# VectorE's residual between the square sums, masks and first exponentials ahead of O's rounding, the value product next to the following scores

## The reference

```python
x = x + 0.5 * ffn(layernorm(x))
x = x + ttt(layernorm(x))          # a sequential linear memory, here "mid"
x = x + 0.5 * ffn(layernorm(x))
```

```python
def _layer(x, ...):
    h = shift_token(x)
    q, k, v = split(h @ wqkv)                    # 256 -> 3 x 512
    q, k = rotary_xpos(l2norm(q) * qs, l2norm(k) * ksc)
    o = local_attention(q, k, v)                 # own and previous 128 tokens
    x = x + o @ wo
    h = layernorm(shift_token(x)) * lg + lb
    a, g = split(h @ w1 + b1)
    x = x + (a * gelu(g)) @ w2 + b2
```

## Time and profile before

| | us |
|---|---|
| median of 3 runs (2850.06 to 2856.06) | 2854.98 |
| time of the profiled execution | 2850.51 |
| span of the profiled execution, first to last instruction | 2848.6 |
| PE matmul busy | 2547.3 (89%) |
| PE weight load busy | 2224.7 (78%) |
| DVE busy | 1987.4 (70%) |
| ACT busy | 1843.2 (65%) |
| POOL busy | 1528.3 (54%) |
| mean granted TensorE clock, share of full | 0.996 |

### The profile page before, as it was taken

The page is one execution under the profiler, slowest core; times in us unless marked ns, Lnnn a source line. Parts: engine busy times, 40 slices in busy tenths (PEclk is TensorE's granted clock), DMA queues, the critical chain, the costliest instruction groups (busy, mean ns, idle before and its releaser), DMA issues.

```text
span 2848.6 us, 79930 instructions
## 1 busy us (share of the span) xinstructions
PE 2547.3 (89%) x29664; PEld 2224.7 (78%) x29664; DVE 1987.4 (70%) x6533; ACT 1843.2 (65%) x5192; POOL 1528.3 (54%) x1767
## 2 busy tenths in 40 slices
PE   7898888998888898899999888899988888999898
PEld 6787777887777787788767777788777777788778
DVE  6776677676767666677656767676766677777776
ACT  5766666666666666666454666666666666666665
POOL 5565556555555556555213555555564555555654
PEclk9999999999999999999999999999999999999999
DMA  3122011003000000004100000000003000000000
GB/s 112 31 76 72 30 34 46 24 19 109 13 2 2 2 2 24 2 2 173 46 23 25 2 2 2 2 2 2 2 2 108 32 2 17 17 17 17 17 17 24
DMA packets 75954, 82.18 MB, mean 29 GB/s; under 512 B 37552, under 2 KB 61872, under 8 KB 74416
## 3 DMA queue, kind: packets, MB, share of 16 engines
q1 hardware_dynamic: 70176, 75.51, 8.1%
q10 hardware_dynamic: 5392, 1.56, 0.2%
HBM read 49.53 MB, written 26.74 MB: 27 GB/s over the span
## 4 chain that ended last, share of the span: by engine, by line
PE 38%; DVE 19%; ACT 18%; POOL 11%; issue 9%; DMA 4%; SPq 2%; DVEq 0%; ACTq 0%; POOLq 0%
PE bank L1111 6%; PE bank L1113 5%; PE bank L1112 5%; POOL pr L631 5%; PE bank L1222 5%; ACT pT L834 5%; DVE pr L1714 5%; ACT pr L815 4%; PE bank L1147 3%; PE bank L1345 3%; DMA stt<-stt 2%; PE bank L1191 2%; POOL r L626 2%; PE bank L1510 2%; POOL r L618 2%
## 5 line engine op out<-in xcount | busy, mean ns | idle before, releaser
L631 POOL TENSOR_TENSOR pr<-pr,rden 128x384 f32<-128x384 f32 (+1 forms) x512 | 435.9, 859 | 645.3 <-DVE rden L1723 644.6
L815 ACT ACTIVATE pr<-pr,nb 128x192 f32<-128x192 f32 (+1 forms) x1024 | 439.1, 430 | 92.3 <-DVE nb L1714 92.3
L1714 DVE CUSTOM_DVE_ANT_0 pr<-bank,maskb,r 128x192 f32<-128x192 f32 (+1 forms) x1024 | 357.3, 395 | 102.5 <-POOL r L626 59.9
L1111 PE MATMUL bank<-h2T,w 128*128 128x256 f32 x1408 | 405.3, 288 | 10.1 <-DVE h2T L1749 4.8
L1112 PE MATMUL bank<-h2T,w 128*128 128x256 f32 x1408 | 394.8, 280 | 0.0
L1113 PE MATMUL bank<-h2T,w 128*128 128x256 f32 x1408 | 394.8, 280 | 0.0
L1111 PE MATMUL bank<-wqkv,hT 128*128 128x512 f32 x768 | 321.3, 418 | 60.5 <-DVE nb L1714 55.4
L663 POOL TENSOR_TENSOR uTl<-t,uTh 128x256 fp32r<-128x256 f32 x288 | 218.0, 757 | 211.4 <-ACT uTh L911 210.6
L1811 DVE SCALAR_TENSOR_TENSOR t<-bank,b,t 128x256 f32<-128x256 f32 (+1 forms) x384 | 182.8, 480 | 185.2 <-ACT t L896 103.0
L1112 PE MATMUL bank<-wqkv,hT 128*128 128x512 f32 x768 | 304.0, 396 | 0.0
L1113 PE MATMUL bank<-wqkv,hT 128*128 128x512 f32 x768 | 302.8, 394 | 0.0
(11 more groups left out here) (244 smaller groups left out, 7362.9 us busy)
## 6 DMA issues: line engine op xcount, KB each, us to landing
wqkv<-wqkv_split SPq DMA_DIRECT2D x18, 512.0 KB, 6.5
w<-w_split SPq DMA_DIRECT2D x3, 2816.0 KB, 9.6
Y<-in_x SPq DMA_DIRECT2D x8, 512.0 KB, 7.3
out<-Y SPq DMA_DIRECT2D x8, 512.0 KB, 3.6
stt<-stt SPq DMA_DIRECT2D x224, 3.0 KB
h<-out SPq DMA_DIRECT2D x7, 512.0 KB, 5.0
out<-h SPq DMA_DIRECT2D x7, 512.0 KB, 3.0
stt<-stt SPq DMA_DIRECT2D x192, 0.0 KB
```

The lines of the kernel that those rows point to most:

```text
L631: e.tensor_tensor(probs(j, t), probs(j, t), rden[:, 2 * j:2 * j + 2].unsqueeze(2).to_broadcast([P, 2, w]), ALU.mult).then_inc(pn_done, 1)
L815: last = e.activation(probs(j, t)[:, g, :], probs(j, t)[:, g, :], ACT.Exp, bias=nb[:, hd:hd + 1], scale=-1.0, accum_out=den[:, hd:hd + 1])
L1111: e.matmul(out, left[0], right[0], start=first, stop=False)
L1714: m = e.tensor_tensor_reduce(probs(j, t)[:, g, :], bank[j][:, g * 256:g * 256 + w], far, r[:, t, 1, place(hd):place(hd) + 1], FAR, ALU.add ...
```

## The change

No instruction of arithmetic is added or removed. Six edits move calls:

1. ACT: the two copies into `o_sum` become a function `O_first`. It runs ahead of `S(0)` of the next tile as before, but the rounded high part `O` now follows `S(0)`.
2. DVE: `O` (the low part) moves from between `S(0)` and `S(1)` to behind `S(3)`; `LN_moments` of tile 3 moves with it, from behind `S(1)`.
3. DVE: `WO(t-1)`, the residual, moves from behind `A0` to between the square sums of k and of q.
4. PE: `A2` (k and q turned) now runs ahead of `PV` instead of behind it.
5. PE: the table `cuts` is another one. The units in `fill(0)`, `fill(1)` and `fill(2)` were 0, 6 and 6 for t = 0 (5 more stand ahead of `S`, as before), 0, 11 and 6 for t = 1 and 2, and 0, 8 and 9 for t = 3. Now they are 4, 8 and 0, then 4, 13 and 0, and 4, 5 and 8.
6. ACT: `A2` (kT and qT copied) of tile 3 moves ahead of `O` and `H2T`.

```diff
--- before.py
+++ after.py
@@ -834,6 +834,15 @@
                         last = e.activation(pTe[64 * a:64 * a + 64, g::2, :], halves_of[64 * g:64 * g + 64, :, a, :], ACT.Copy)
                 last.then_inc(pt_sb, 1)
 
+            def O_first(L, b, t):
+
+                n = idx(L, b, t)
+                e.wait_ge(o_lo, at(o_lo, 2 * n))
+                e.wait_ge(pv_ps, at(pv_ps, 2 * n + 2))
+                for i in pair:
+                    cols = slice(2 * P * i, 2 * P * i + 2 * P)
+                    e.activation(o_sum[:, cols], bank[O_BANK[0]][:, cols], ACT.Copy).then_inc(o_first, 1)
+
             def O(L, b, t):
 
                 n = idx(L, b, t)
@@ -843,11 +852,6 @@
                         e.wait_ge(pv_ps, at(pv_ps, 2 * n + i + 1))
                         e.activation(oT[:, 0, 2 * i:2 * i + 2, :].rearrange("p a c -> p (a c)"), bank[O_BANK[i]][:, 0:2 * P], ACT.Copy).then_inc(o_hi, 1)
                 else:
-                    e.wait_ge(o_lo, at(o_lo, 2 * n))
-                    e.wait_ge(pv_ps, at(pv_ps, 2 * n + 2))
-                    for i in pair:
-                        cols = slice(2 * P * i, 2 * P * i + 2 * P)
-                        e.activation(o_sum[:, cols], bank[O_BANK[0]][:, cols], ACT.Copy).then_inc(o_first, 1)
                     e.wait_ge(wo_ps, at(wo_ps, n))
                     for i in pair:
                         e.wait_ge(o_added, at(o_added, sums(L, b, t) + i + 1))
@@ -918,10 +922,12 @@
                 for t in range(NT):
                     ahead = (L, b, t + 1) if t < NT - 1 else nxt and (*nxt, 0)
                     ahead2 = (L, b, t + 2) if t < NT - 2 else nxt and (*nxt, t - 2)
-                    if t:
-                        O(L, b, t - 1)
+                    if t > 1:
+                        O_first(L, b, t - 1)
                     for j in range(3):
                         S(L, b, t, j)
+                        if t and j == 0:
+                            O(L, b, t - 1)
                     if t == 0:
                         A1_k(*ahead)
                     S(L, b, t, 3)
@@ -935,11 +941,12 @@
                         PTE(L, b, t)
                     if ahead2:
                         A0(*ahead2)
+                    if ahead:
+                        A2(*ahead)
                     if t == 3:
+                        O_first(L, b, t)
                         O(L, b, t)
                         H2T(L, b, 0)
-                    if ahead:
-                        A2(*ahead)
                     if L == 0 and b < B - 1 and 0 < t < 3:
                         for k in (2 * t - 2, 2 * t - 1):
                             entry_apply(b + 1, k)
@@ -1350,7 +1357,7 @@
                 for t in range(NT):
                     ahead = (L, b, t + 1) if t < NT - 1 else nxt and (*nxt, 0)
                     ahead2 = (L, b, t + 2) if t < NT - 2 else nxt and (*nxt, t - 2)
-                    cuts = ((5, 5, 11, UNITS), (0, 0, 11, UNITS), (0, 0, 11, UNITS), (0, 0, 8, UNITS))[t]
+                    cuts = ((5, 9, UNITS, UNITS), (0, 4, UNITS, UNITS), (0, 4, UNITS, UNITS), (0, 4, 9, UNITS))[t]
 
                     def fill(k):
                         if prev and cuts[k] < cuts[k + 1]:
@@ -1379,13 +1386,13 @@
                     fill(1)
                     if ahead2:
                         A0(*ahead2)
+                    if ahead:
+                        A2(*ahead, 0)
+                        A2(*ahead, 1)
                     if t:
                         PV(L, b, t)
                     else:
                         PV_first(L, b, t)
-                    if ahead:
-                        A2(*ahead, 0)
-                        A2(*ahead, 1)
                     fill(2)
                     if t == 3:
                         H2T(L, b, 0)
@@ -1919,14 +1926,14 @@
                     S(L, b, t, 0)
                     if t > 1:
                         O_add(L, b, t - 1, 1)
-                    if t:
-                        O(L, b, t - 1)
                     S(L, b, t, 1)
-                    if t == 3:
-                        LN_moments(L, b, 0)
                     S(L, b, t, 2)
                     R(L, b, t, 0)
                     S(L, b, t, 3)
+                    if t:
+                        O(L, b, t - 1)
+                    if t == 3:
+                        LN_moments(L, b, 0)
                     if prev and t:
                         W2(*prev, t - 1)
                     for j in range(1, 4):
@@ -1945,6 +1952,7 @@
                             entry_stats(b + 1, j)
                     if ahead and t:
                         squares(idx(*ahead), 0)
+                        WO(L, b, t - 1)
                         squares(idx(*ahead), 1)
                         rotary(*ahead, 1)
                         rotated(*ahead, 1)
@@ -1959,7 +1967,8 @@
                     if ahead2:
                         A0(*ahead2)
                     if t:
-                        WO(L, b, t - 1)
+                        if not ahead:
+                            WO(L, b, t - 1)
                         halves(L, b, t - 1)
                     if L == 0 and b == 0 and t < 3:
                         split_lo(4 + t)
```

## The result

The changed kernel takes **3175.49 us** (median of 4 runs, 3172.16 to 3178.29), the one before 2852.52 (4 runs, 2849.32 to 2856.06): ratio **1.1131, 95% interval [1.1112, 1.1151]**, 323 us slower. The forecast was 3100 with a range of 2975 to 3200.

The account below looks back on a forecast made before the run. PE, busy 89%, was taken as the bound, so its waits matter. The profiled 2850.5 us plus 137 for the filler's wait and 117 for the clock gave 3104, put at 3100 as layer 0 loses slightly less; range 2975 to 3200.

Parts of the forecast that it names:

- the place and the cause: Filler ahead of A1, tiles 1 to 3: PE waits for DVE's addition, about 90 times 3.3 to 4.2 us, 330 us.
- Rival C: The wait for xf_done is already met at fill(0), so the gains stand alone: 2738 us; chance 3%.
- A: Rival: the wait before A1 is as worked out but the clock stays up: 2988 us; chance 20%.
- D: Rival: the gate costs far less, so that tile 3 pays nothing: about 2900 us; chance 6%.
- the payback: A1 3.9 us later in tile 2, mostly repaid by vanished waits: scores to scores 0.85 us slower, tile 1 1.09.
- the two first sequences: The two sequences without a prev have no filler and so only the gain, estimated at -11 us.
- the length of the waits: PE standing still ahead of A1: 3.3 us in tile 1, 3.6 in tile 2, 4.2 in tile 3.
- I take 1.3: Clock loss in A1 behind each wait, between 0 and 2.5 us, taken as 1.3: 90 x 1.3 = +117 us.
- most are nearer to 3.4 than to 4.2, and a part of the fall can lie in the wait itself: Reason given for taking the clock loss per wait ahead of A1 well under 2.5 us.
- Rival B: Every wait ahead of A1 brings the clock down at the full 2.5 us: 3213 us; chance 14%.
- what the edits would give by themselves: Residual, mask pass 1 and A2 moved: about 2 us each in tiles 1 and 2, net some 3.5 a sequence.
- tile 3 gives some back: In tile 3 A2 waits for POOL's scaling of k with PV queued behind it, reducing the net to 3.5 us.

Follow-up runs that it names:

- e2: Kernel before with only four filler units moved between scores and projections in tiles 1 to 3: 3322.15 us, ratio 1.1645.
- e3: Changed kernel with DVE's addition of the previous filler product called ahead of O_add and the mask passes, filler left in place: 2783.92 us, ratio 0.976.
- e4: Changed kernel with 32 transposes of the identity on PE ahead of the waiting filler in tiles 1 to 3, results unread: 3020.44 us, ratio 1.0591.
- experiment 155: Not a run number: the 155 us by which e4, the changed kernel with 32 added transposes, is faster than the changed kernel; e4 measured 3020.44 us.
- e10: Kernel before with only DVE's residual WO moved between the square sums of k and q: 2731.31 us, ratio 0.9573.
- e5: e3 with the old order in tile 3 alone (PV ahead of A2, ScalarE's O and H2T ahead of kT and qT): 2703.8 us, ratio 0.9488.
- e9: Changed kernel with 12 transposes on PE ahead of the waiting filler, where e4 has 32: 3068.57 us, ratio 1.0758.

## Why the prediction was right, and where its sizes were off

**Right: the place and the cause.** The filler's first matmul does wait for the addition that DVE makes behind mask pass 3 of the same tile, 90 times (355 us, 330 forecast). e2 shows the cost with nothing else changed, e3 shows that it goes when the addition comes earlier. Rival C (the addition is no obstacle) fails, and so does A (the clock stays up): it would be e4's kernel, and the changed one is 155 us slower. D (tile 3 pays nothing) fails too, since tile 3 pays 3.6 us.

**Right: the payback.** Of a late start of 3.9 us, one us a tile was to remain. Tile 1: 16.55 to 16.63 measured, 16.66 forecast; tile 2: 17.1 against 17.0 (e4). DVE's and PE's rows carried that sum well. With the clock up, everything together comes to +169 instead of +137 (e4). The rows of e4 divide the 32 us. Tile 3 is 3.6 us longer instead of 3.0, some 18 us in 30 sequences, and tile 0 is 0.16 longer instead of not at all, 5 us. The other 11 us are the two first sequences, which were to gain them and gained nothing (0.1 us longer and 0.1 shorter). Their tiles 1 and 2 did become 1.6 to 3.6 us shorter, but tile 3 became 3.4 and 5.3 longer, and tile 0 of the very first 1.8. `A2` stands ahead of `PV` there too, filler or not, and waited 3.0 us for POOL; the sum had put this at nothing. The waits of `A2` in e4:

```profile
PE bank L1154 <- POOL t L621: 108.9, 67, 3.0
```

**Slightly off: the length of the waits.** I took the addition at 4.8 us behind the scores, it came at 5.03, so PE stands still for 3.96 and 4.5 us instead of 3.6 and 4.2 in tiles 2 and 3 (3.4 for 3.3 in tile 1). My sum took off 0.2 us for a wait for ScalarE, but from the first mask pass to the addition it is 3.96 us instead of 4.02.

**Mis-sized: "I take 1.3", the clock's part.** Forecast 90 x 1.3 = 117; the rows of the trace give 182, the experiment 155. The difference is mostly paid back in tile 3. Against e4, tiles 1 and 2 of the changed kernel are 1.6 and 2.0 us longer in the mean, all that `A1` loses there, but tile 3 only 1.2 of its 2.5: `A2` comes later there and waits less for POOL, 80 us in all instead of 109. The step that failed is "most are nearer to 3.4 than to 4.2, and a part of the fall can lie in the wait itself". Two thirds of the waits were of 4.0 us or more, and all of these brought the clock down. A part of the fall does lie in the wait (the granted clock is 0.75 in its last 3 us, in the window below), but PE still came out of it at half clock and ran so for 5 us (1160.79 to 1166). That window:

```profile
1158.00:1161.00 3.00, 0.21 (x1) 0.24 (x2) 2.72 (x15) 3.00 (x14) 1.03 (x2) 0.75 0.00 0
```

Rival B's 2.5 each was right for tile 3 alone (2.40 to 2.53). The Trainium skill (TensorE: Matmul & The Clock Gate, "HAM oscillation - how this bites in real kernels") describes a kernel that waits in every step and starts cold in every one of them. For waits of 3.4 us and more the rows here agree, 85 of 88.

**Wrong: "what the edits would give by themselves", 3.5 us a sequence or 112 us.** e3, the change with the wait taken out, gives 67 us. The residual is worth more than thought (119 alone, e10), while `A2` ahead of `PV` in tile 3 takes 80 (e5). I had written "tile 3 gives some back", and had not worked out that `A2` would stand there for 2.4 us with `PV` behind it. This carried rival C's 2738, and the same oversight is behind the 11 us of the two first sequences. That a gain of 5% lay in the same edits, with one call moved and tile 3 left alone, was not seen.

## What to carry to other kernels

When filler work goes into a gap of an engine that takes its queue in order, look up what its first instruction waits for and where, in the same stretch, that is made: if it is made later than the gap, the filler is a gate for all behind it, and its producer has to move with it. Count the clock beside the wait: with stops of 3.4 us or more ahead of dense matmuls, 155 of 323 us here were half clock in the matmuls behind them, and stops of 1.9 us already brought it down in 13 of 30 cases. And try the edits of a batch one by one, since here one gave 119 us, one took 80, and one took over 370.

## What was not expected of the hardware

- Stops of PE of 1.9 us brought the granted clock to half in 13 of 30 cases, 2.5 us in 9 of 30, 3.0 us in 18 of 28 (e9), 3.4 in 27 of 30, 4.0 and more in 58 of 58. Ahead of `A2` in tile 3, stops of 2.44 us did so in 14 of 28 cases (e3) and of 1.8 us in 5 of 26 (e4). Equal stops of 1.91 us went either way.
- The mean loss grew with the stop, 1.67, 2.05 and 2.40 us, though the matmuls behind it were the same; the fall can also set in only some matmuls after PE has resumed, as at 299.11 in e9. What decides it was not tried.
- Matmuls whose result nobody reads, in the time of the stop, take the loss away: no projections at half clock behind the 90 stops, clock 0.992 instead of 0.919, and 155 us (e4).
